# The softplus of a state-space scan: two products of quadratics replaced by three chained squares and two wide VectorE operations

## The reference

```python
u, z = jnp.split(x @ in_w.T, 2, axis=-1)            # 256 channels each
u = jax.nn.silu(conv of u over 4 tokens + conv_b)
dbc = u @ xproj_w.T
dt = jax.nn.softplus(dbc[..., :dt_rank] @ dt_w.T + dt_b)
Bm, Cm = ...                                         # 16 states each
dA = jnp.exp(dt[..., None] * A)
dBu = (dt * u)[..., None] * Bm[:, :, None, :]
h = dA_t * h + dBu_t ;  y_t = sum over n of h * C_t
return (y + u * D) * jax.nn.silu(z) @ out_w.T
```

## Time and profile before

| | |
|---|---|
| runs | 1466.38 us median of 3 (1465.43 to 1467.89) |
| profiled execution, span from first to last instruction | 1437.5 us |
| TensorE busy | 1295.8 us (90%) |
| VectorE busy | 1180.6 us (82%) |
| GpSimd busy | 1063.1 us (74%) |
| ScalarE busy | 954.9 us (66%) |

### The profile page before, as it was taken

One profiled execution on the slowest core, in us unless ns is written; L12 is line 12 of the kernel. 1 busy time (PEld: TensorE's weight loads), 2 busy tenths in 40 slices (PEclk: granted clock), 3 DMA queues, 4 the chain that ended last, 5 costly groups with the idle time before them and its releaser, 6 DMA issues.

```text
span 1437.5 us, 26311 instructions
## 1 busy us (share of the span) xinstructions
PE 1295.8 (90%) x9310; PEld 959.2 (67%) x9310; DVE 1180.6 (82%) x1941; ACT 954.9 (66%) x1762; POOL 1063.1 (74%) x668
## 2 busy tenths in 40 slices
PE   6799999999999999999999777998998999998995
PEld 3566666666666666666666655568997666666993
DVE  6889999999999999999999995433335788977776
ACT  6968977987887887797787784224555555453343
POOL 2989999999999999999999992531333466565573
PEclk9999999999999999999999998999999999999998
DMA  6123323322332322332332223231214200002233
GB/s 205 68 93 116 103 87 116 113 92 101 113 104 97 117 106 107 116 112 78 116 112 99 91 96 143 101 98 41 84 53 146 94 2 2 1 17 57 77 95 105
DMA packets 53873, 132.03 MB, mean 92 GB/s; under 512 B 8369, under 2 KB 33457, under 8 KB 44033
## 3 DMA queue, kind: packets, MB, share of 16 engines
q1 hardware_dynamic: 48976, 120.56, 24.2%
q0 software_dynamic: 4768, 9.81, 2.1%
HBM read 117.40 MB, written 18.56 MB: 95 GB/s over the span
## 4 chain that ended last, share of the span: by engine, by line
PE 39%; DVE 33%; issue 10%; ACT 8%; POOL 6%; DMA 2%; SPq 1%; DVEq 0%; POOLq 0%; ACTq 0%
DVE hh L900 16%; DVE hh L890 7%; DVE hh L871 4%; PE pq L396 3%; PE pa L498 3%; PE bank L1512 2%; PE bank L1522 2%; PE bank L1508 2%; PE py L519 2%; PE pr L2169 2%; PE bank L1428 2%; POOL hc L1049 2%; POOL ytoken L2029 2%; PE bank L1418 2%; PE bank L1419 1%
## 5 line engine op out<-in xcount | busy, mean ns | idle before, releaser
L1049 POOL TENSOR_TENSOR hc<-hh,cs 128x1024 f32<-128x1024 f32 x256 | 599.0, 2369 | 43.5 <-DVE hh L890 40.8
L519 PE MATMUL py<-ident,hc 128*128 128x128 f32 x2048 | 270.6, 276 | 27.7 <-ACT yt L730 22.7
L519 PEld LDWEIGHTS py<-ident,hc 128*128 128x128 f32 x2048 | 233.5, 142 | 89.1 <-issue 42.3
L900 DVE TENSOR_TENSOR_SCAN hh<-pa,st,hh 128x512 f32<-128x512 f32 x240 | 288.9, 1262 | 1.5 <-ACT pa L710 0.8
L710 ACT ACTIVATE pa<-dt,w 128x512 f32<-128x512 f32 x320 | 212.0, 683 | 56.3 <-DVE hh L900 51.7
L890 DVE TENSOR_TENSOR_SCAN hh<-da,st,pa 128x512 f32<-128x512 f32 x144 | 175.5, 1259 | 4.0 <-PE pa L498 2.7
L498 PEld LDWEIGHTS pa<-dg,dtut 64*128 64x128 f32 x1536 | 96.2, 189 | 85.2 <-issue 81.5
L498 PE MATMUL pa<-dg,dtut 64*128 64x128 f32 x1536 | 113.6, 286 | 40.4 <-DVE hh L900 36.2
L871 DVE TENSOR_TENSOR hh<-dtu,pb 128x1024 f32<-128x1024 f32 x112 | 134.3, 1199 | 1.3 <-PE pb L465 1.2
L465 PE MATMUL pb<-crow,sel 128*128 128x512 f32 x224 | 122.2, 628 | 9.6 <-DVE hh L871 9.5
L705 ACT ACTIVATE da<-dt,w 128x512 f32<-128x512 f32 x192 | 127.0, 712 | 0.0
(11 more groups left out here) (343 smaller groups left out, 2879.7 us busy)
## 6 DMA issues: line engine op xcount, KB each, us to landing
cs<-bcrows SPq DMA_DIRECT2D x64, 1024.0 KB, 4.7
bs<-bcrows SPq DMA_DIRECT2D x48, 256.0 KB, 3.6
xsorted<-in_pads SPq DMA_DIRECT2D x13, 387.0 KB, 5.4
rot<-in_rot SPq DMA_DIRECT2D x4, 1024.0 KB, 4.9
wx<-in_l_w SPq DMA_DIRECT2D x4, 1024.0 KB, 11.3
ysort<-ytoken SPq DMA_DIRECT2D x14, 256.0 KB, 4.8
wx<-in_l_w SPq DMA_DIRECT2D x1, 3072.0 KB, 11.3
wx<-in_l_w SPq DMA_DIRECT2D x1, 2304.0 KB, 17.8
```

The lines of the kernel that those rows point to most:

```text
L519: i = pe.matmul(py[:, h * CH + kt * P:h * CH + (kt + 1) * P], hc[s % HCS][:, h, t], ident[:, :], is_transpose=True, start=n == 0 and kt == ...
L900: v.tensor_tensor_scan(hh[s % HHS][:, h, :], pa[i % SLOTS][:, :], hh[s % HHS][:, h, :], 0.0 if first else st[:, m % 2, n, h:h + 1], ALU.mu ...
L1049: g.tensor_tensor(hc[s % HCS][:, :, :], hh[s % HHS][:, :, :], cs[j % 2][:, s % CG, :].unsqueeze(1).broadcast_to([P, HF, CH]), ALU.mult).th ...
```

## The change

The polynomial is made in another way: three squares chained, each of the scaled and shifted result of the one before, all on ScalarE and each 128x1024 (both halves at once). The first reads `ab` and writes `ww`, the second works in `ww`, the third writes into a pair of PSUM banks. VectorE then needs two operations of 128x1024: `softplus_log` adds a constant and multiplies by s (at n = 11), `softplus_sum` scales and adds the relu (at n = 12).

```diff
-SPREAD = 0.7285826634011618
-FACTORS = ((0.9233720474324719, 0.5983295270873473), (-0.5618955766453696, 1.062684925042419))
+SQUARES = ((0.0879134100057549, 1.0659627042897553), (0.920087862624148, -1.0733253113649461), (79.981268034486, 1.5529501443353244))
...
-                    order = [("square", 0, f, h) for f in range(2) for h in range(HF)] + [("relu", 0, h) for h in range(HF)]
+                    order = [("square", 0, h) for h in range(HF)] + [("relu", 0, h) for h in range(HF)]
...
-                        if m + 1 < UNITS and n in (10, 11):
-                            order += [("square", m + 1, n - 10, h) for h in range(HF)]
+                        if m + 1 < UNITS and n == 11:
+                            order += [("square", m + 1, h) for h in range(HF)]
                         if m + 1 < UNITS and n == 12:
                             order += [("relu", m + 1, h) for h in range(HF)]
...
                     def square(m, f):
-                        act.wait_ge(s_zz, 2 * m + 2)
-                        for h in range(HF):
-                            i = turn["square", m, f, h]
+                        act.wait_ge(s_zz, len(SQUARES) * m + f + 1)
+                        source, scale, bias = ab if f == 0 else ww, SQUARES[f][0], keep[:, NCH + f:NCH + f + 1]
+                        if f < len(SQUARES) - 1:
+                            act.activation(ww[:, :, :], source[:, :, :], ACT.Square, scale=scale, bias=bias).then_inc(s_zz, 1)
+                        else:
+                            i = turn["square", m, 0]
                             if i >= SLOTS:
-                                act.wait_ge(s_taken, free(i))
-                            act.activation(pa[i % SLOTS][:, :], ww[:, h, :], ACT.Square, scale=SPREAD,
-                                           bias=keep[:, NCH + f:NCH + f + 1]).then_inc(s_slot, 1)
+                                act.wait_ge(s_taken, free(i + 1))
+                            act.activation(pa2[i // 2 % (SLOTS // 2)][:, :], flat(source[:, :, :]), ACT.Square, scale=scale,
+                                           bias=bias).then_inc(s_slot, HF)
...
-                            if n == 8:
-                                z_squared(m)
-                            if n in (9, 10):
-                                square(m, n - 9)
+                            if n in (8, 9, 10):
+                                square(m, n - 8)
                             if n == 11:
                                 relu_again(m)
...
-                    def finish(m):
-                        for h in range(HF):
-                            i = turn["relu", m, h]
-                            v.wait_ge(s_slot, slot_count(i))
-                            v.wait_ge(s_taken, turn["square", m, 1, h] + 1)
-                            v.tensor_tensor(dt[m % 2][:, h, :], pa[i % SLOTS][:, :], dt[m % 2][:, h, :], ALU.add).then_inc(s_taken, 1)
+                    def softplus_log(m):
+                        i = turn["square", m, 0]
+                        v.wait_ge(s_slot, slot_count(i + 1))
+                        v.scalar_tensor_tensor(flat(dt[m % 2][:, :, :]), pa2[i // 2 % (SLOTS // 2)][:, :], LOG_OFFSET, flat(ab[:, :, :]),
+                                               ALU.add, ALU.mult).then_inc(s_taken, HF)
+
+                    def softplus_sum(m):
+                        i = turn["relu", m, 0]
+                        v.wait_ge(s_slot, slot_count(i + 1))
+                        v.wait_ge(s_taken, turn["square", m, HF - 1] + 1)
+                        v.scalar_tensor_tensor(flat(dt[m % 2][:, :, :]), flat(dt[m % 2][:, :, :]), LOG_SCALE, pa2[i // 2 % (SLOTS // 2)][:, :],
+                                               ALU.mult, ALU.add).then_inc(s_taken, HF)
...
                     def prep(m, n):
                         if m < UNITS:
-                            if n in (10, 11):
-                                factor(m, n - 10)
+                            if n == 11:
+                                softplus_log(m)
                             if n == 12:
-                                finish(m)
+                                softplus_sum(m)
```

More of the change, by code:

```diff
@@ L40 @@
 LAG = 4
-SPREAD = 0.7285826634011618
-FACTORS = ((0.9233720474324719, 0.5983295270873473), (-0.5618955766453696, 1.062684925042419))
-LN2 = 0.6931471805599453
+SQUARES = ((0.0879134100057549, 1.0659627042897553), (0.920087862624148, -1.0733253113649461), (79.981268034486, 1.5529501443353244))
+SHIFT = -0.8206125682501487
+LOG_SCALE = 0.12443449
+LOG_OFFSET = 1.94734153 / LOG_SCALE
 W_U = 0
@@ L221, in layer0_mamba @@
             s_op, s_om = sem("out_projected"), sem("out_kept")
-            s_zz = sem("sigmoid_and_its_square")
+            s_zz = sem("sigmoid_and_its_squares")
             with ExitStack() as k:
@@ L228, in layer0_mamba @@
                 lnp = sb(k, "lnp", [P, 2])
-                keep = sb(k, "keep", [P, NCH + len(FACTORS) + 1])
+                keep = sb(k, "keep", [P, NCH + len(SQUARES) + 1])
                 sel = sb(k, "sel", [P, NS])
@@ L630, in sigmoid @@
                         act.activation(ab[:, :, :], ab[:, :, :], ACT.Sigmoid, scale=-1.0,
[L631 to L636, removed]
+                                       bias=keep[:, NCH + len(SQUARES):NCH + len(SQUARES) + 1]).then_inc(s_zz, 1)
                     def square(m, f):
-                        act.wait_ge(s_zz, 2 * m + 2)
-                        for h in range(HF):
-                            i = turn["square", m, f, h]
+                        act.wait_ge(s_zz, len(SQUARES) * m + f + 1)
[4 more added lines that the diff above has]
+                            i = turn["square", m, 0]
                             if i >= SLOTS:
-                                act.wait_ge(s_taken, free(i))
-                            act.activation(pa[i % SLOTS][:, :], ww[:, h, :], ACT.Square, scale=SPREAD,
-                                           bias=keep[:, NCH + f:NCH + f + 1]).then_inc(s_slot, 1)
+                                act.wait_ge(s_taken, free(i + 1))
+                            act.activation(pa2[i // 2 % (SLOTS // 2)][:, :], flat(source[:, :, :]), ACT.Square, scale=scale,
+                                           bias=bias).then_inc(s_slot, HF)
                     def relu_again(m):
@@ L781, in mamba_scalar @@
                     sigmoid(0)
-                    z_squared(0)
-                    square(0, 0)
+                    for f in range(len(SQUARES)):
+                        square(0, f)
                     act.wait_ge(s_pre, 4)
-                    square(0, 1)
                     relu_again(0)
@@ L839, in mamba_vector @@
                 def mamba_vector():
-                    def factor(m, f):
-                        for h in range(HF):
-                            i = turn["square", m, f, h]
-                            v.wait_ge(s_slot, slot_count(i))
[L844 to L847, removed]
-                    def finish(m):
-                        for h in range(HF):
-                            i = turn["relu", m, h]
-                            v.wait_ge(s_slot, slot_count(i))
-                            v.wait_ge(s_taken, turn["square", m, 1, h] + 1)
-                            v.tensor_tensor(dt[m % 2][:, h, :], pa[i % SLOTS][:, :], dt[m % 2][:, h, :], ALU.add).then_inc(s_taken, 1)
+                    def softplus_log(m):
[9 more added lines that the diff above has]
+                                               ALU.mult, ALU.add).then_inc(s_taken, HF)
                     def prep(m, n):
                         if m < UNITS:
-                            if n in (10, 11):
-                                factor(m, n - 10)
+                            if n == 11:
+                                softplus_log(m)
                             if n == 12:
-                                finish(m)
+                                softplus_sum(m)
                     def inflow(s):
@@ L983, in mamba_vector @@
                     keep_turned(2)
-                    factor(0, 0)
-                    factor(0, 1)
-                    finish(0)
+                    softplus_log(0)
+                    softplus_sum(0)
                     first_dt_times_u()
@@ L2765, in constants @@
     k = {"ident": np.eye(P, dtype=np.float32)}
-    keep = np.array([c % (NCH // B) > 0 for c in range(NCH)] + [f[0] for f in FACTORS] + [-LN2], np.float32)
+    keep = np.array([c % (NCH // B) > 0 for c in range(NCH)] + [f[1] for f in SQUARES] + [SHIFT], np.float32)
     k["keep"] = np.broadcast_to(keep, (P, len(keep)))
```

## The result

The changed kernel takes 1449.6 us (median of 4 runs, 1447.43 to 1452.68), the one before 1467.14 us on the same chip (4 runs). The ratio is 0.9882 with a 95% interval of 0.9866 to 0.9899: 1.2% faster, 17.5 us. The forecast was 1447.5 us, with 1438 to 1458 as its range.

What follows compares the result with a forecast made beforehand. VectorE was taken to bound the scan, with GpSimd 2 us behind it. 4.8 (first unit) + 3 x 0.85 + 11 x 1.05 = 18.9 us off the 1466.4 us median gave 1447.5 us, range 1438 to 1458.

Steps and rivals of the forecast that it cites:

- What bounds the kernel, and the root of both gaps: Scan unit: VectorE bounds it, busy 50.71 of 51.63 us; its gaps of 0.33 and 0.57 us come from TensorE's late inflow.
- VectorE's own work: Per unit, six 128x512 operations (3.56 us) become two 128x1024 ones at 1.13 us each: VectorE's work falls by 1.30 us.
- TensorE 1.50 us earlier: Step 11 of a unit: TensorE's inflow waits for step 9 instead of step 10, so it starts 1.50 us earlier.
- chain of 7.85 us: From TensorE's inflow of step 11 to ScalarE's copy of the projection: 7.85 us, all moving earlier with that inflow.
- sum at the second relu copy: The one sum needs both relu copies, stalls VectorE 0.8 us, and leaves a gain of 1.05 us per unit.
- the three set apart: Three units that start a batch or follow one that does (second, ninth, tenth): gain of 0.85 us each.
- The first unit, 4.8 us by the clock: First unit: TensorE idles 1.9 us, not 4.17; if the clock holds the sum ends 4.8 us earlier, else gain 1.8.
- The start, put at nothing: Softplus ahead of the scan: its ScalarE chain is some 0.3 us longer, hidden until GpSimd's other rows end at 37.1.
- The 28.9 us above the span: The median of the runs stands 28.9 us above the profile's span, with nothing of it touched by the change.
- VectorE and GpSimd alone as the limit: Rival: relu copies come before VectorE needs them, units shrink to GpSimd's 49.65 us, 1434 us in all; chance 0.13.
- the slower rival: Rival: TensorE doesn't start earlier, the sum ends 0.45 us later in 14 units, 6.3 us, 1473 us; chance 0.07.
- the half gain: Rival: clock falls in the first unit, and GpSimd or step 10's decays take tenths per unit, about 1456 us; chance 0.12.

Runs made afterwards that it cites:

- banks undone: Changed kernel, but TensorE again waits for the scans of step 10 before the inflow of step 11: 1477.17 us, ratio 1.0061.
- after again: Changed kernel run and profiled a second time, without any edit: 1453.96 us, ratio 0.9887.
- banks alone: Kernel before with its first square and factor handed over one step earlier, VectorE's six 128x512 operations kept: 1454.77 us, ratio 0.9904.
- short start: Changed kernel with the middle square of the softplus ahead of the scan made on one column of each half: 1451.34 us (one run).
- first unit undone: Changed kernel with TensorE's wait for step 10 put back in the first unit alone: 1457.12 us (one run).
- halves again: Second measurement of the changed kernel with the sum as two 128x512 operations, each waiting for its own relu copy: 1450.51 us, ratio 0.9858.

## Why the prediction was right

**What bounds the kernel, and the root of both gaps.** Right, and shown from both sides: the gaps go with the order of the banks alone, and come back, larger, when it is undone.

**VectorE's own work, 1.13 us for a wide operation.** Right: the log starts at 634.51 and the next at 635.63, 1.12 us. What this saves is worth nothing by itself (banks undone). It is worth something once nothing else holds the stretch: with the banks' order and narrow operations the unit is 50.73, with wide ones and no other gap 49.61.

**TensorE 1.50 us earlier, chain of 7.85 us, sum at the second relu copy.** Right to 0.1 us, with the pieces a little otherwise: the last softplus, which has no projection in front of it and was left at 1.05, gained 1.38, and one more unit than the three set apart gained only 0.83. From the end of the first unit's sum to the last gate, before took 877.56 - 86.94 = 790.6 us and after 859.68 - 83.3 = 776.4: 14.2 us for the fourteen units, where the prediction's terms for them add to 2.55 + 11.55 = 14.1.

**The first unit, 4.8 us by the clock.** That the clock would hold was right: in after and after again TensorE idles 1.95 us and the clock stays at full rate, and it falls after 4.06 and 4.17. The Trainium skill (TensorE: Matmul & The Clock Gate, Part 1) has it fall after idling; the falls seen here agree. But the prediction's reason, that 1.9 us is nearer to 1.50 than to 4.17, is not borne out. The clock also fell in or right behind idling of 3.13 us (banks alone), of 2.5 to 2.8 us at the start of the scan in both kernels, and of 1.91 us in short start and in banks undone, while it held after 1.84 in first unit undone. The length of the gap alone doesn't decide, so some luck was in it. As to the size, the sum of this unit ended 3.7 us earlier than before, not 4.8. In after again, counted from the first scans, it is 4.8 (46.3 us to the last softplus operation and 1.2 for it in before, 41.6 and 1.1 here).

**The start, put at nothing.** This is the term that was mis-sized. The prediction took a chain longer by 0.3 us and hid it under GpSimd's rows. VectorE's wait for the squares grew by 1.83 us (1.25 to 3.08), because three full squares and no half to begin with stand in front of the log. The product of dt and u came 0.7 us later, and GpSimd, done with its rows at 36.47, waited 0.87 us for it before its first inflow at 37.34, where it had none before. Its rows had ended 0.6 us earlier than before, so the first inflow and the first scans came only 0.3 us later (39.73 for 39.45). The other 0.8 us lie between the first scans and the first unit's sum and come with the clock: in after, TensorE's first inflow takes 2.08 us and its second starts 8.3 us behind the first scans; in after again, with the same instructions, they are 1.16 and 7.3. Whether the longer chain makes the worse of the two likelier is not shown. These 0.3 and 0.8 us make the difference between 18.9 us forecast and 17.9 seen at the last gate (877.56 to 859.68), less the 0.1 that the fourteen units gave above their terms.

**The 28.9 us above the span.** Wrong, without harm to the result: nearly all of them were not around the instructions but a wait near the end that the first profiled execution lacked. The forecast took its 18.9 us off the median of the runs, and nothing in it depended on that reading. The forecast for the span of the new profile did: 1418.6 us, where 1447.7 came.

**The rivals.** VectorE and GpSimd alone as the limit did not come, since the relu copy held the sum; with that removed and the square moved, GpSimd is what is left (49.61 us by the unit, forecast 49.65). TensorE did start earlier, so the slower rival did not come either, and GpSimd had its 0.9 us to spare, against the half gain.

## What to carry to other kernels

When a ring of buffers joins engines, look up which earlier item each filler waits for before you count the operations saved: here a handed item less between two scans moved a wait to an older one, and that alone was 0.90 of 1.05 us per unit. One wide operation in the place of two saves a start, but it waits for the last of its inputs; where they come one after the other, halves can be the faster form. And take a span against the run's time in a second profile before you explain the difference.

## What was not expected of the hardware

In the last mixture of experts VectorE and ScalarE each wait 18 to 31 us in total for a releaser that the profile calls remote, in every profile but the first. After again and halves again had another such wait of 9 to 15 us in the first mixture, and they are the two in which what follows the scan took 599 us. What these waits are was not tried. What follows the scan took between 588 and 599 us from one profile of the edited kernels to the next, which is more than some of the edits are worth.

TensorE's clock fell to its lower level right behind 1.91 us of idling (short start, banks undone) and held after 1.95 (after, and four other profiles, before step 11 of the first unit).
